# Moving the value's scaling in the second pass from VectorE to ScalarE and GpSimd

## What is computed

```python
Vg = u.reshape(b, s, H, HD) * (vp * u_gate)[..., None]     # the value: u times one coefficient per head
def step(Sc, inp):                                         # H = 32 heads of HD = 16, two components S0, S1
    a11, a12, bt, k, v = inp
    r0 = a11[..., None] * S0 + a12[..., None] * S1
    r1 = -a12[..., None] * S0 + a11[..., None] * S1
    Sr = jnp.stack([r0, r1], -1)
    err = v - jnp.sum(k * Sr, -1)                          # the value is needed here
    Sn = Sr + bt[..., None, None] * err[..., None] * k
    return (Sn, Sn)
_, Y = jax.lax.scan(step, S0, xs)
y = jnp.sum(Q * Y, -1).reshape(b, s, DI)
```

## Time and profile before

| what | us |
|---|---|
| median of three runs | 1533.96 |
| lowest, highest | 1533.52, 1534.76 |
| the profiled execution's own time | 1534.93 |
| its span, first to last instruction | 1533.2 |
| DVE busy | 1185.5 (77%) |
| PE busy | 1265.2 (83%) |
| ACT busy | 514.8 (34%) |
| POOL busy | 173.4 (11%) |

### The profile page before, as it was taken

The page is one execution under the profiler, slowest core; times in us unless marked ns, Lnnn a source line. Parts: engine busy times, 40 slices in busy tenths (PEclk is TensorE's granted clock), DMA queues, the critical chain, the costliest instruction groups (busy, mean ns, idle before and its releaser), DMA issues. The chain is left out here.

```text
span 1533.2 us, 13155 instructions
## 1 busy us (share of the span) xinstructions
PE 1265.2 (83%) x4244; PEld 745.1 (49%) x4244; DVE 1185.5 (77%) x1957; ACT 514.8 (34%) x1174; POOL 173.4 (11%) x77
## 2 busy tenths in 40 slices
PE   5950888645988786896899999899987696999997
PEld 2530333222555454453556666565554463666664
DVE  5889999889999877689899999869999774510011
ACT  3752111000223464565523232321232653332332
POOL 0000244401122100000001111002222000000000
PEclk9985999977999898798899999999999897999999
DMA  4000111010311122100123321312111102432221
GB/s 165 1 7 14 55 55 55 0 55 14 110 47 50 43 87 110 63 1 7 50 101 96 96 97 55 110 69 97 55 42 41 55 1 83 162 124 82 69 82 68
DMA packets 52116, 98.73 MB, mean 64 GB/s; under 512 B 4689, under 2 KB 40018, under 8 KB 50898
## 3 DMA queue, kind: packets, MB, share of 16 engines
q1 hardware_dynamic: 52050, 97.91, 18.3%
HBM read 75.87 MB, written 22.02 MB: 64 GB/s over the span
## 5 line engine op out<-in xcount | busy, mean ns | idle before, releaser
L649 PE MATMUL ps<-kz 128*128 128x256 f32 x1024 | 245.2, 383 | 14.4 <-ACT kz L889 12.7
L635 PE MATMUL ps<-kz 128*128 128x512 f32 x512 | 246.2, 605 | 4.5 <-DVE coef L1077 2.5
L649 PEld LDWEIGHTS ps<-kz 128*128 128x128 f32 x1024 | 196.0, 192 | 97.6 <-issue 61.1
L540 PE MATMUL ps<-wshare,uT 128*128 128x512 f32 x512 | 226.8, 596 | 2.7 <-DVE work L1466 2.7
L889 ACT ACTIVATE kz<-ps,small 128x512 f32<-128x512 f32 x128 | 87.6, 686 | 305.9 <-PE ps L635 305.7
L464 PE MATMUL ps<-wshare,xnT 128*128 128x512 f32 x256 | 120.1, 613 | 64.3 <-ACT ps L713 64.3
L540 PEld LDWEIGHTS ps<-wshare,uT 128*128 128x128 f32 x512 | 95.4, 191 | 111.4 <-issue 108.2
L635 PEld LDWEIGHTS ps<-kz 128*128 128x128 f32 x512 | 99.5, 195 | 83.5 <-issue 75.0
L943 POOL TENSOR_TENSOR work<-work 128x1024 f32<-128x1024 f32 x28 | 66.9, 2389 | 641.6 <-DVE work L1363 402.9
L790 ACT ACTIVATE kz<-ps 128x128 f32<-128x128 f32 x128 | 33.6, 277 | 292.5 <-PE ps L525 292.5
L959 POOL TENSOR_TENSOR kz<-work 128x1024 f32<-128x1024 f32 x32 | 76.3, 2383 | 384.0 <-DVE work L1489 384.0
(11 more groups left out here) (264 smaller groups left out, 2022.8 us busy)
## 6 DMA issues: line engine op xcount, KB each, us to landing
kz<-in_w SPq DMA_DIRECT2D x128, 256.0 KB, 3.0
kap_d<-kz SPq DMA_DIRECT2D x26, 512.0 KB, 2.7
kz<-kap_d SPq DMA_DIRECT2D x26, 512.0 KB, 3.2
uT<-in_x SPq DMA_DIRECT2D x8, 512.0 KB, 5.5
wshare<-in_wq SPq DMA_DIRECT2D x2, 2048.0 KB, 7.7
kz<-in_x SPq DMA_DIRECT2D x2, 2048.0 KB, 7.9
coef<-in_x SPq DMA_DIRECT2D x2, 2048.0 KB, 7.8
wshare<-in_wk SPq DMA_DIRECT2D x2, 1024.0 KB, 11.1
```

What stands on the lines that cost most here:

```text
L540: t = mm(ps[:, 2 * (j % 2) + c, :], uT3[:, k, j * P:(j + 1) * P], wq_s[:, k, c, :], start=(k == 0), stop=(k == KI - 1))
L635: t = mm(ps[:, 4 + i % 2, :], w1_r[r][:, k, (f % 2) * P:(f % 2 + 1) * P], x2T[:, k, n * 512:(n + 1) * 512], start=(k == 0), stop=(k == KM ...
L649: t = mm(ps[:, 6 + q // 2, (q % 2) * DM:(q % 2 + 1) * DM], hbuf(i)[:, q * P:(q + 1) * P], w2_r[r][:, f % 2, :], start=(f == 0 and q % 2 == ...
```

## The change

`value` is taken out of DVE. Two instructions on other engines stand in its place: ACT copies u as it is out of PSUM into the value's tile (`raw_value`), and POOL multiplies the tile by the coefficient in place (`value`, a 128x512 multiplication). `ut_used`, on which `token_u` waits, is now counted up by ACT's copy. DVE waits for the new semaphore `v2_ready` ahead of e. The tiles and their number stay as they are; line numbers of the kernel after are 15 to 22 higher in this region.

```diff
+        def vh(j):
+            return wshare[:, 4096:4608] if j % 2 else tmp[:, 4096:4608]
...
@@ ScalarE, passes(b)
+                act.wait_ge(scan_done, b + 1)
+                raw_value(b, 0)
+                raw_value(b, 1)
                 for j in range(L):
                     act.wait_ge(yt_ready, b * L + j + 1)
...
                     t.then_inc(yt_done, 1)
+                    if j + 2 < L:
+                        raw_value(b, j + 2)
...
+            def raw_value(b, j):
+                act.wait_ge(ut_ready, 2 * L * b + L + j + 1)
+                if j >= 2:
+                    act.wait_ge(k2_used, b * L + j - 1)
+                af(vh(j), ps[:, 4 + j % 2, :], ACT.Copy).then_inc(ut_used, 1)
@@ GpSimd
+            def value(b, j):
+                pool.wait_ge(ut_used, 2 * L * b + L + j + 1)
+                cv = cf[:, CV, j].unsqueeze(2).to_broadcast([P, H, HD])
+                w = vh(j).rearrange("p (h d) -> p h d", h=H)
+                nc.gpsimd.tensor_tensor(w, w, cv, ALU.mult).then_inc(v2_ready, 1)
...
+                value(b, 0)
                 for j in range(L):
                     pool.wait_ge(kq_used, 2 * L * b + L + j + 1)
...
                     nc.gpsimd.tensor_tensor(qb(j), w[0], w[1], ALU.add).then_inc(turned_ready, 1)
+                    if j + 1 < L:
+                        value(b, j + 1)
@@ VectorE, pass_2(b)
-                def value(j):
-                    dve.wait_ge(ut_ready, 2 * L * b + L + j + 1)
-                    tt(by_head(vh[j % 2], 0), by_head(ps[:, 4 + j % 2, :], 0), wide(cf[:, CV, j]), MUL).then_inc(ut_used, 1)
...
-                value(0)
...
-                    if j + 1 < L:
-                        value(j + 1)
                     after(at["e"])
-                    dve.wait_ge(ut_used, 2 * L * b + L + j + 1)
-                    e = vh[j % 2]
+                    dve.wait_ge(v2_ready, b * L + j + 1)
+                    e = vh(j)
```

More of the change, by code:

```diff
@@ L217, in build @@
         turned_ready = sem("turned_ready")
+        v2_ready = sem("v2_ready")
         yp_ready = sem("yp_ready")
@@ L1451, in pass_2 @@
                 Y = tmp[:, 3072:4096].rearrange("p (i n) -> p i n", i=2)
-                vh = [tmp[:, 4096:4608], wshare[:, 4096:4608]]
                 at = {}
-                def value(j):
-                    dve.wait_ge(ut_ready, 2 * L * b + L + j + 1)
-                    tt(by_head(vh[j % 2], 0), by_head(ps[:, 4 + j % 2, :], 0), wide(cf[:, CV, j]), MUL).then_inc(ut_used, 1)
                 def turn(j):
```

## The result

The kernel after takes 1610.55 us in the median (1609.44 to 1612.86) against 1534.36 us before. The ratio is 1.0497, with a 95% interval of 1.0479 to 1.0516. It is slower, inside the predicted range (1570 to 1618) and 6 us above the predicted 1605.

A forecast was written before the change was run, and what follows sets the result against it. DVE bounds the kernel before; PE, waiting for ACT, was to bound it after. Batch 0's pass +21.6 us, batch 1's +22.9, clock +26: +71 on 1534.9, or 1606, less 1.0 to the median: 1605 us, range 1570 to 1618.

The forecast's parts named there:

- PE waits for ACT's y work: Before token_u from token 4 on: PE waits for ACT's y and copy, gap 2.97 us for 1.04, step 12.28 us.
- The start of the chain: Batch 0: token 4's token_u starts at 387.88, after ACT's y of token 0 and the copy.
- The clock: Behind PE's gaps: clock lost in four of six at 1.8 us, 1.2 us a gap on average, 26 us in all.
- The end of a pass: From the end of the last projection to the end of the pass: 23.5 us.
- The port: POOL's multiplication and DVE's SBUF work exclude each other: 1.18 us a step added to DVE, its step 10.93 us.
- only the port counts: Rival: ACT's copy frees the bank in time, DVE's 10.93 us step sets the pace, +17, 1551 us; chance 0.06.
- What `value` was worth: In DVE's step of 10.35 us: `value` takes 0.60 us, 18 us over 30 steps.
- The loop of DVE and POOL: Multiplication to multiplication: 11.8 us, barely hidden behind PE's 12.28; rival that it is longer, 1620 to 1645 us, chance 0.05.
- Faster: Rival: neither the bank nor the port binds, DVE loses 30 x 0.60 us, 1516 us; chance 0.04.

The follow-up runs named there:

- copy_only: Against the kernel after: ACT's copy stays behind the y work, POOL has no multiplication, DVE multiplies in SBUF right before the error; 1608.75 us.
- copy_first: Against the kernel after: ACT's copy of token j + 2 stands ahead of its wait for turn_y(j); 1540.95 us, ratio 1.0041 to before.
- filled_gap_3: Against the kernel after: PE does three extra matmuls right before token_u of tokens 4 to 15, waits unchanged; 1576.86 us.
- act_scales: Against the kernel after: copy ahead of the y work, ACT scales while copying, one instruction per head, POOL's multiplication dropped; 1518.81 us, ratio 0.9910 to before.
- copy_between: Against the kernel after: ACT's copy stands between the four copies and four squares of its y work; 1553.39 us, ratio 1.0138 to before.

## Why the prediction was right, step by step

- *PE waits for ACT's y work.* Right: 2.96 us for the predicted 2.97, 24 times, released by the copy. copy_only shows that this alone makes the loss, and copy_first that without it 70 of 76 us are gone.
- *The start of the chain.* Token 4's `token_u` starts at 388.85, or 387.92 without the 0.93 us by which the pass began later; 387.88 was worked out.
- *The clock.* Right in kind, too small in size. I took four gaps in six and 1.8 us each, 1.2 on average, for a step of 13.5 us. In truth all twelve gaps of batch 0 are followed by work at the lower clock, and a step is 13.77 us on average, 1.49 more than 12.28. So the clock was lost more often than I said and a loss cost less; that the product came near was in part luck. 11 x 0.29 = 3.2 us of batch 0's pass were missing. The sum also counts 22 gaps where there are 24: it leaves out the last of each pass, behind which the last projection ends 8.9 us after `token_u` starts (540.30 to 549.20) and not 7.5, another 1.4 us. With the end of the pass 0.7 us too long (next point) that is 3.9 us, the whole difference between 21.6 + 11 x 1.2 = 34.8 and the measured 38.7. Over both passes: +71 predicted on the profiled execution, +77.8 in the span. Taken together the clock was priced at 26 us, and filled_gap_3 measures 34.
- *The end of a pass.* 23.5 us were predicted from the last projection to the last `product`. L544's last entry ends at 549.20 and the pass at 572.00: 22.8.
- *The port.* Right that the multiplication and DVE's SBUF work exclude each other, and that it isn't what sets the time. Both terms of the sum for "only the port counts" were off: the multiplication takes 1.06 us and not 1.18, it costs DVE 0.73 and not all of its length (in copy_first's rows its last 1.06 us begin at 456.51, 0.17 before the error starts, and the error ends 0.54 behind it, 0.15 less than its own 0.69), and DVE gains 0.47 and not 0.60. The net is +0.26 us a step, where +0.58 was predicted. That rival's 1551 us would have been 1541.
- *What `value` was worth.* 0.60 was read from the starts of L1457 and L1499. But `value` stood between L1493 and the error that needs its result, and so seems to have covered a delay between the two. Without it L1512 and L1516 of act_scales start 0.88 apart and not 1.38 - 0.60 = 0.78, and the error's follower 0.73 behind it and not 0.71. These two rows make 0.12 of the 0.13 us between 9.88 and 9.75. That the delay comes from the dependence is argued from the order of the instructions; no run varied it.
- *The loop of DVE and POOL.* 11.8 us was to fit under PE's step. It did: from the end of the multiplication at 459.37 to the end of the next L1512 at 471.20 are 11.8 us, and then DVE waits for the value.
- *Faster.* Refuted for this change. But the 1516 us that was named for it is about what the two versions reach that have neither the wait nor the port (1519.88 and 1518.81).

What stays open: why 3 of 24 gaps of 1.86 us cost clock in copy_between and the other 21 don't. The unchanged code ahead of L590 (L586 before, L595 with the filled gap) asks the same. PE's gap there is 2.97 to 3.02 us at two places of each kernel. In 17 of the 20 cases of this record nothing is lost, and in three the clock is, both of them in the kernel after and one in filled_gap_3:

```profile
627.11 8.83 PE L590 MATMUL ps<-wo_s,work 128*128 128x256 f32 x32 [2.98 <-DVE kz L1544]
...
1337.09 8.83 PE L590 MATMUL ps<-wo_s,work 128*128 128x256 f32 x32 [2.97 <-DVE kz L1544]
```

The earlier trace rows has the same two at 7.14. So a share counted on six gaps of one trace, four in six, was a weak base for these 24. No run was made to tell what decides.

## What to carry to other kernels

When an instruction moves to another engine, the question is not only whether that engine has time, but what stands ahead of it in that engine's order, and who is released by it. Here the copy on an engine with two thirds of its time free stood behind 2.3 us of work that PE's instruction just before had started, and so tied PE to ACT in every step. A wait in PE's stream can cost more than its length, since the work behind it may run at half clock (2.96 us idle and another 1.4 to 1.7 us lost here). And work given to GpSimd from VectorE cost VectorE time beside its instructions with both operands in SBUF (0.73 us a step for a multiplication of 1.06 us), and none beside `turn`, which reads PSUM. Where ScalarE does it, even in 32 small pieces, VectorE's rows stay as they are (0.69 us for the error, a step of 9.88 us, the same as with hardly any multiplication).

## What the runs showed of the hardware that I had not expected

- Small ScalarE instructions follow each other every 0.17 us (128x16, PSUM to SBUF, each with its own scale per partition), so 512 elements in 32 pieces cost 5.4 us against 0.58 in one.
- All 24 gaps of 2.96 us cost clock, where the trace of before had four in six for gaps of that size. Three of 24 gaps of 1.86 us did as well. At the two unchanged places ahead of L590 it was three in 20. The length of a gap alone does not tell it.
- 5.2 us of useless matmuls in a gap of 2.96 us made the kernel only 13 us slower over 24 steps (1623.63 for 1610.55), and 2.6 us of them made it 34 us faster.
- An instruction between two dependent ones on VectorE is partly free: `value` took 0.60 us of the step, and its removal gave 0.47 (9.88 for 10.35).
